# Ten of sixteen tiles transposed by DMA from SyncE, two V weight groups interleaved, and every load of the first stage in one queue

## The reference

```python
def reference(x, w_q, w_k, w_v, w_o, w_gate, w_up, w_down):   # x: 4 x 2048 x 2048, f32
    x = x + _layernorm(attn(_layernorm(x), w_q, w_k, w_v, w_o))
    x = x + _layernorm(ffn(_layernorm(x), w_gate, w_up, w_down))
    return x
# attn: q, k, v = x @ w_q.T, x @ w_k.T, x @ w_v.T; 16 heads of 128;
#       softmax(q k^T / sqrt(128)) v, then @ w_o.T
# ffn:  (silu(x @ w_gate.T) * (x @ w_up.T)) @ w_down.T, 8192 hidden channels
```

## Time and profile before

| | us |
|---|---|
| median of three runs | 2283.08 |
| all three runs | 2280.57, 2641.86, 2283.08 |
| the profiled execution, its own time | 2280.66 |
| its span, slowest core (core 6) | 2278.8 |
| spans of the eight cores | 2276.7 to 2278.8 |
| PE busy in the span | 2240.6 (98%) |

### The profile page before, as it was taken

One profiled execution on the slowest core, in us unless ns is written; L12 is line 12 of the kernel. 1 busy time (PEld: TensorE's weight loads), 2 busy tenths in 40 slices (PEclk: granted clock), 3 DMA queues, 4 the chain that ended last, 5 costly groups with the idle time before them and its releaser, 6 DMA issues.

```text
span 2278.8 us, 26636 instructions; the slowest of 8 cores (2276.7 to 2278.8 us)
## 1 busy us (share of the span) xinstructions
PE 2240.6 (98%) x10528; PEld 1018.2 (45%) x10528; DVE 573.4 (25%) x771; ACT 567.8 (25%) x743; POOL 132.9 (6%) x252
## 2 busy tenths in 40 slices
PE   5999999999999999999999999999999999999998
PEld 3544444444444444444444444444444444444443
DVE  6400045454554557601000001010000000000005
ACT  4411266666666651200000000000000000000003
POOL 0000000000000000000000000000000010000000
PEclk9999999999999999999999999999999999999999
DMA  9720021411414157654444444444444374445447
GB/s 265 162 44 2 10 35 22 75 28 32 71 23 71 28 111 187 164 93 74 75 80 77 74 75 80 78 74 75 79 78 74 65 145 68 83 66 86 72 83 258
DMA packets 61689, 190.49 MB, mean 84 GB/s; under 512 B 21632, under 2 KB 21632, under 8 KB 56448
## 3 DMA queue, kind: packets, MB, share of 16 engines
q0 software_dynamic: 36864, 134.27, 35.8%
q1 hardware_dynamic: 8064, 50.34, 6.3%
q10 hardware_dynamic: 16640, 4.20, 1.0%
HBM read 302.06 MB, written 16.78 MB: 140 GB/s over the span
## 4 chain that ended last, share of the span: by engine, by line
PE 96%; DMA 1%; issue 1%; ACT 1%; DVE 1%; DVEq 0%; SPq 0%; ACTq 0%; POOLq 0%
PE ps L167 96%; DMA wvs<-wv 1%; DMA xs<-xb 1%; ACT kt L173 0%; DVE st L232 0%; ACT pt L170 0%; ACT pvc L173 0%; DVE xn L240 0%; ACT x L170 0%; ACT sdv L170 0%; ACT ln1t L173 0%; SPq L164 0%; DVE x L831 0%; DVE fs L814 0%; DVEq L849 0%
## 5 line engine op out<-in xcount | busy, mean ns | idle before, releaser
L167 PE MATMUL ps<-ln3t,we 128*128 128x512 bf16 x3872 | 835.9, 379 | 0.0
L167 PEld LDWEIGHTS ps<-ln3t,we 128*128 128x128 bf16 x3872 | 378.9, 98 | 456.8
L167 PE MATMUL ps<-ln1t,w 128*128 128x512 bf16 x1536 | 371.7, 379 | 3.3 <-ACT kt L173 3.3
L170 ACT ACTIVATE pt<-ps,kon 128x1024 bf16<-128x1024 f32 x256 | 285.1, 1115 | 190.4 <-PE ps L167 190.4
L170 ACT ACTIVATE sil<-ps 128x512 f32<-128x512 f32 x128 | 76.3, 597 | 780.0 <-PE ps L167 779.6
L167 PEld LDWEIGHTS ps<-ln1t,w 128*128 128x128 bf16 x1536 | 148.1, 98 | 190.1 <-issue 15.5
L167 PE MATMUL ps<-wvs,ln1t 128*128 128x512 bf16 x1024 | 225.3, 381 | 6.3 <-DMA wvs<-wv 6.3
L167 PE MATMUL ps<-ring,ga 128*128 128x512 bf16 x1024 | 222.1, 379 | 0.4
L167 PE MATMUL ps<-ring,gb 128*128 128x512 bf16 x1024 | 221.7, 379 | 0.0
L167 PEld LDWEIGHTS ps<-wvs,ln1t 128*128 128x128 bf16 x1024 | 100.0, 98 | 125.6 <-issue 9.3
L167 PEld LDWEIGHTS ps<-ring,ga 128*128 128x128 bf16 x1024 | 100.0, 98 | 121.9 <-issue 1.8
(11 more groups left out here) (59 smaller groups left out, 895.2 us busy)
## 6 DMA issues: line engine op xcount, KB each, us to landing
ring<-wd POOLq DMA_DIRECT2D x64, 512.0 KB, 6.0
we<-wu POOLq DMA_DIRECT2D x61, 512.0 KB, 5.9
we<-wg POOLq DMA_DIRECT2D x60, 512.0 KB, 6.0
xs<-xb SPq DMA_DIRECT2D x16, 1024.0 KB, 14.8
wvs<-wv POOLq DMA_DIRECT2D x16, 512.0 KB, 11.9
w<-wq POOLq DMA_DIRECT2D x16, 512.0 KB, 6.1
w<-wk POOLq DMA_DIRECT2D x16, 512.0 KB, 6.0
xr<-xb SPq DMA_DIRECT2D x8, 1024.0 KB, 7.1
```

Of the source, the lines that this page charges most:

```text
L167: return op("t", lambda e: e.matmul(dst, lhsT, rhs, start=start, stop=stop), ctr)
L170: return op("s", lambda e: e.activation(dst, src, fn, bias=bias, scale=scale), ctr)
```

## The change

It does the following:

- Tiles 6 to 15 are no longer transposed by PE and ACT. DVE writes them into a ring of four buffers XNB, and SyncE issues a DMA transpose of each (`x_transpose_dma`) from XNB into LN1T. From tile 10 on the norm waits until the transpose four tiles back has landed.
- x is loaded by GpSimd, in one queue with the weights. The weights of groups 0 and 1 no longer wait for a tile of x; their place in the list sets their order. SyncE issues nothing in this stage but the ten transposes.
- PE multiplies tiles 0 to 5 with group 0, then tiles 0 to 3 with group 1 piece by piece, and then in turn tile k of group 0 and tile k-2 of group 1. The first two tiles of group 2 are done piece by piece.
- From tile 6 on DVE does the first block of the next tile's statistics while it waits for the square root. The order before, in which from tile 7 on the whole statistics of a tile stood ahead of the norm of the tile before it (`x_norm_behind`), is gone.

```diff
--- before.py
+++ after.py
@@ -91,6 +91,7 @@
     XS = [at("xs%d" % i, o, 2048, F32) for i, o in enumerate(
         (OT_O, OT_O + 8192, OT_O + 16384, VT_O + 49152, VT_O + 57344))]
     XN = at("xn", OT_O + 24576, 4096, BF16)
+    XNB = at("xnb", VT_O + 32768, 8192, BF16)
     W = at("w", W_O, 6144, BF16)
     WV = at("wvs", R_O, 16384, BF16)
     KT = at("kt", R_O, 4096, BF16)
@@ -181,7 +182,6 @@
 
     dI = C("dI")
     vK = C("vK")
-    k_ident = dma("g", IDENT.r(0, 128), idn[:, :], dI)
     op("v", lambda e: e.memset(ONES.r(0, 128), 1.0))
     op("v", lambda e: e.memset(KON.r(0, 1), EPS))
     k_const = op("v", lambda e: e.memset(KON.r(1, 1), -SH), vK)
@@ -199,6 +199,7 @@
     sSD = C("sSD")
     vRS = C("vRS")
     vXN = C("vXN")
+    dLT = [C("dLT%d" % i) for i in range(4)]
     tT = C("tT")
     sT = C("sT")
     tV = C("tV")
@@ -210,8 +211,8 @@
 
     def x_load(tc):
         if tc >= 5:
-            wt("y", xnorm[tc - 5])
-        x_in[tc] = dma("y", XS[tc % 5].r(0, 2048), xb[tc * 128:(tc + 1) * 128, :], dX[tc % 5])
+            wt("g", xnorm[tc - 5])
+        x_in[tc] = dma("g", XS[tc % 5].r(0, 2048), xb[tc * 128:(tc + 1) * 128, :], dX[tc % 5])
 
     def row_aggr(p):
         wt("v", (vB, vB.n))
@@ -225,21 +226,36 @@
         wt("v", rs)
         return rs
 
-    def x_stats(tc):
+    def x_stats(tc, blocks):
         p, xs = tc % 2, XS[tc % 5]
         wt("v", x_in[tc], aggr.get(tc - 2))
-        for c in range(4):
+        for c in blocks:
             op("v", lambda e, c=c: e.bn_stats(ST.r(p * 24 + c * 6, 6), xs.r(c * 512, 512)), vB)
+
+    def x_norm(tc):
+
+        p, xs = tc % 2, XS[tc % 5]
+        x_stats(tc, range(1 if tc >= 7 else 0, 4))
         aggr[tc] = row_aggr(p)
-
-    def x_norm(tc):
-        p, xs = tc % 2, XS[tc % 5]
+        if 6 <= tc < NTC - 1:
+            x_stats(tc + 1, range(1))
         row_rstd(p, aggr[tc])
-        if tc >= 2:
-            wt("v", xt_pe[tc - 2])
+        if tc >= 6:
+            dst = XNB.r((tc - 6) % 4 * 2048, 2048)
+            wt("v", lnt.get(tc - 4) if tc >= 10 else None)
+        else:
+            dst = XN.r(p * 2048, 2048)
+            wt("v", xt_pe.get(tc - 2))
         xnorm[tc] = op("v", lambda e: e.tensor_scalar(
-            XN.r(p * 2048, 2048), xs.r(0, 2048), MV.r(p * 2, 1), SDV.r(p * 2 + 1, 1),
+            dst, xs.r(0, 2048), MV.r(p * 2, 1), SDV.r(p * 2 + 1, 1),
             ALU.subtract, ALU.mult), vXN)
+
+    def x_transpose_dma(tc):
+
+        wt("y", xnorm[tc])
+        lnt[tc] = op("y", lambda e: e.dma_start(
+            LN1T(tc * 128, (2048, NKC), (1, 128)), XNB.r((tc - 6) % 4 * 2048, 2048), transpose=True),
+            dLT[tc % 4], 16)
 
     def x_transpose(tc):
         if tc == 0:
@@ -259,12 +275,10 @@
 
     wv_in = {}
 
-    def wv_load(g, after=(None, None, None, None)):
-
-        for c in range(4):
+    def wv_load(g, chunks=range(4)):
+        for c in chunks:
             if g >= 2:
                 wt("g", v_pe[(NTC - 1, g - 2)])
-            wt("g", after[c])
             wv_in[(g, c)] = dma("g", WV.r((g % 2) * 8192 + c * 2048, 2048), wv[g, c, :, :], dWV[g % 2][c])
 
     v_pe = {}
@@ -303,55 +317,85 @@
         src = wq if m % 2 == 0 else wk
         w_in[m] = dma("g", W.r((m % 3) * 2048, 2048), src[m // 2, :, :], dW[m % 3])
 
-    def x_norm_behind(tc):
-
+
+    x_load(0)
+    k_ident = dma("g", IDENT.r(0, 128), idn[:, :], dI)
+    for c in range(4):
+        x_load(c + 1)
+        wv_load(0, [c])
+
+    def x_next(tc):
         if tc < NTC:
-            x_stats(tc)
-        x_norm(tc - 1)
-        if tc + 4 < NTC:
-            x_load(tc + 4)
-
-    for tc in range(5):
-        x_load(tc)
-    wv_load(0, [x_in[tc] for tc in range(4)])
-
-    def x_at_once(tc):
-        x_stats(tc)
-        x_norm(tc)
-        x_load(tc + 5)
-
-
-    for tc in range(4):
-        x_at_once(tc)
+            x_norm(tc)
+            if tc + 5 < NTC:
+                x_load(tc + 5)
+
+
+    x_next(0)
+    x_transpose(0)
+    x_next(1)
+    v_part(0, 0, 0)
+    x_transpose(1)
+    x_next(2)
+    v_part(1, 0, 0)
+    for tc in (2, 3):
+        for t in range(tc - 1):
+            v_part(t, 0, tc - 1)
         x_transpose(tc)
-        if tc:
-            for t in range(tc):
-                v_part(t, 0, tc - 1)
-            for c in range(tc):
-                v_part(tc, 0, c)
-    x_at_once(4)
-    x_transpose(4)
-    x_at_once(5)
-    for t in range(4):
+        x_next(tc + 1)
+        v_part(tc - 1, 0, tc - 1)
+        for c in range(tc):
+            v_part(tc, 0, c)
+    for t in range(2):
         v_part(t, 0, 3)
         v_out(t, 0)
-    for k in range(4, NTC):
-        if k == 4:
-            x_at_once(6)
-            x_stats(7)
-        elif k + 3 <= NTC:
-            x_norm_behind(k + 3)
-        if k + 1 < NTC:
-            x_transpose(k + 1)
+    x_transpose(4)
+    x_next(5)
+    for t in range(2, 4):
+        v_part(t, 0, 3)
+        v_out(t, 0)
+    v_part(4, 0, 0)
+    v_part(4, 0, 1)
+    v_part(4, 0, 2)
+    x_transpose(5)
+    wv_load(1, [0])
+    x_next(6)
+    x_transpose_dma(6)
+    v_part(4, 0, 3)
+    v_out(4, 0)
+    wv_load(1, [1, 2, 3])
+    for tc in range(7, 10):
+        x_next(tc)
+        x_transpose_dma(tc)
+        if tc == 7:
+            v_proj(5, 0)
+        else:
+            for t in range(4):
+                v_part(t, 1, tc - 8)
+    for c in (2, 3):
+        for t in range(4):
+            v_part(t, 1, c)
+            if c == 3:
+                v_out(t, 1)
+    for k in range(6, NTC):
+        if k + 4 < NTC:
+            x_next(k + 4)
+            x_transpose_dma(k + 4)
         v_proj(k, 0)
-    wv_load(1, [x_in[tc] for tc in (7, 9, 11, 13)])
-    wt("g", x_in[NTC - 1])
+        v_proj(k - 2, 1)
     for m in range(3):
         w_load(m)
-    for g in (1, 2, 3):
-        if g >= 2:
-            wv_load(g)
-        for tc in range(NTC):
+    for k in (NTC - 2, NTC - 1):
+        v_proj(k, 1)
+    for g in (2, 3):
+        wv_load(g)
+        if g == 2:
+            for c in range(4):
+                for t in range(2):
+                    v_part(t, g, c)
+            v_out(0, g)
+            v_out(1, g)
+        for tc in range(2 if g == 2 else 0, NTC):
             v_proj(tc, g)
```

More of the change, by code:

```diff
@@ L226, in row_rstd @@
         return rs
-    def x_stats(tc):
+    def x_stats(tc, blocks):
         p, xs = tc % 2, XS[tc % 5]
         wt("v", x_in[tc], aggr.get(tc - 2))
-        for c in range(4):
+        for c in blocks:
             op("v", lambda e, c=c: e.bn_stats(ST.r(p * 24 + c * 6, 6), xs.r(c * 512, 512)), vB)
-        aggr[tc] = row_aggr(p)
     def x_norm(tc):
         p, xs = tc % 2, XS[tc % 5]
+        x_stats(tc, range(1 if tc >= 7 else 0, 4))
+        aggr[tc] = row_aggr(p)
+        if 6 <= tc < NTC - 1:
+            x_stats(tc + 1, range(1))
         row_rstd(p, aggr[tc])
-        if tc >= 2:
-            wt("v", xt_pe[tc - 2])
+        if tc >= 6:
[4 more added lines that the diff above has]
+            wt("v", xt_pe.get(tc - 2))
         xnorm[tc] = op("v", lambda e: e.tensor_scalar(
-            XN.r(p * 2048, 2048), xs.r(0, 2048), MV.r(p * 2, 1), SDV.r(p * 2 + 1, 1),
+            dst, xs.r(0, 2048), MV.r(p * 2, 1), SDV.r(p * 2 + 1, 1),
             ALU.subtract, ALU.mult), vXN)
+    def x_transpose_dma(tc):
[3 more added lines that the diff above has]
+            dLT[tc % 4], 16)
     def x_transpose(tc):
```

## The result

The changed kernel takes **2315.43 us**, median of 13 executions (lowest 2288.23), against 2283.08 us before (2280.57 the lowest). The ratio is **1.0109, 95% interval 1.0077 to 1.014**: within 2% as forecast, but the time is 29 us above the predicted 2286.6 us and outside 2274 to 2296.

A forecast was written before the change was run, and what follows sets the result against it. PE (98% busy) bounds the kernel, DMA the first stage to about 55 us. Tile 6 at 79.4 us, 1.7 of clock, 186.6 of sums and 0.8 end the stage at 268.5 against 265.0: +3.5, forecast 2286.6 us, range 2274 to 2296.

The forecast's parts named there:

- Loads and w_v: First stage: 3.1 us per load, group 1's first piece at 54.9 us, PE waiting about 8 us from near 47 us.
- Tile 6's transpose: First stage: starved packet for packet beside loads, landing at 79.4 us when PE needs it at 72.2 us.
- The 0.4 us for the signal in the sum: Added for the signal to the landing time of tile 6's DMA transpose, 79.4 us.
- DVE, tile 15, weights of group 2: After tile 6: DVE idle before tile 10's norm, tile 15 and weights loading from about 83 us, 0.8 us exposed for group 2.
- The stage's end: End of the first stage, where the next one's first matmul starts: 268.5 us against 265.0, +3.5 us.
- Slow clock. I charge 1.7 us once.: PE at 1.2 GHz behind the wait for tile 6: 1.7 us once, between 0 and 3 us possible.
- pacing by the transposes: Rival, first stage: 11.7 us per transpose, one following the other, sets PE's pace; +45 us, 2328 us; chance 0.04.
- another wait: Rival: an unseen wait, such as DVE or SyncE held by a full ring at 80 to 100 us; +8 to +20 us; chance 0.11.
- Transposes in time: Rival: tile 6 landed by 72.2 us without holding up loads, stage ending at 259.6 us; -5.4 us, 2277.7 us; chance 0.28.

The follow-up runs named there:

- after_again: The changed kernel run again unaltered, to trace an execution with a long pair of cores; 2319.74 us, ratio 1.0132.
- hold_loads: Changed kernel with loads of tiles 12 to 15, and q and k weights behind them, held until tile 9's transpose landed; 2284.55 us, 1.0004.
- busy_pe: Changed kernel with 28 and 30 idle matmuls filling PE's waits for group 1's first piece and tile 6's transpose; 2287.91 us, 1.003.
- busy_second: Changed kernel with 30 idle matmuls only where PE waits for tile 6's transpose; 2288.95 us, 1.004.
- pe_all: Changed kernel with all sixteen tiles transposed by PE, none by DMA in the stage; load order and single queue kept; 2285.96 us, 1.0017.
- dma_from_10: Changed kernel with tiles 6 to 9 transposed by PE and only tiles 10 to 15 by DMA; 2286.87 us, 1.0019.
- dma10_late_w: Changed kernel with only tiles 10 to 15 transposed by DMA, q and k weights loaded only behind tile 15's transpose; 2280.56 us, 0.9989.
- dma10_act: As dma10_late_w, but the six DMA transposes issued from ACT's queue in place of SyncE's; 2281.22 us, 0.9986.
- pe_all_gap: pe_all with one added PE wait, for tile 14's load ahead of tile 6's sum with group 0; 2292.42 us, 1.0036.
- busy_first: Changed kernel with 28 idle matmuls only where PE waits for group 1's first piece; 2312.98 us, 1.0116.
- after_mixed: Changed kernel with 16 idle PE transpositions behind each of the first six pairs of sums after the wait for tile 6's transpose; 2317.1 us, 1.0119.
- hold_wait: hold_loads with an added PE wait for tile 9's DMA transpose ahead of tile 6's sum with group 0; 2320.59 us, 1.018.
- pe_all_wait6: pe_all with PE waiting for tile 14's load ahead of the last piece of group 1 of tile 1, earlier than pe_all_gap; 2319.64 us, 1.0164.
- before_gap: Kernel before the change with one added PE wait, for tile 14's load ahead of tile 7's first sum; 2298.01 us, 1.0072.
- before_two_gaps: Kernel before the change with two added PE waits: tile 10's load ahead of tile 5's first sum, tile 14's ahead of tile 7's; 2300.68 us, 1.0083.
- pe_all_wait7: pe_all_gap with PE waiting for tile 15's load in place of tile 14's; 2299.04 us, 1.0073.
- hold_wait_long: hold_wait with PE waiting for tile 12's load in place of tile 9's transpose; 2297.28 us, 1.0087.
- dma10_wait7: dma_from_10 with an added PE wait for tile 15's load ahead of tile 6's sum with group 0; ratio 1.0093.

## Why the prediction was wrong

Step by step, on the profiled execution's slowest core:

- **Loads and w_v.** First piece of group 1 predicted at 54.9 us, PE went on at 56.8; loads took 3.2 us each, the upper bound I had kept. PE's wait was 6.0 us, not 8: it came to it later, held up by ACT's copies between the first tiles (4.9 us in six waits), which I had counted at nothing. Nearly right.
- **Tile 6's transpose.** Predicted: issued at 46.3, landed at 79.4 by one packet for one and a dry queue at the end, PE waiting about 7 us. Measured: issued at 49.0, landed at 80.0, wait 6.7 us, 271 packets against 269. Right, in cause and size. (The 0.4 us for the signal in the sum has no row behind it, and no run measures it alone.) The Trainium skill's page "DMA: Bandwidth & Descriptors", section "SWDGE vs HWDGE vs iDMA", names packets of preferably up to 4096 bytes as the point where an engine changes queue; read as sixteen of the transpose's records per turn, that would have given no wait. The trace disagrees with this reading: a turn was one packet of some 250 bytes (0.25 MB in 1026).
- **DVE, tile 15, weights of group 2.** DVE idle before tile 10's norm 5.4 us, q and k weights issued from 82.6 us, the transposes from tile 8 on landing in 4.6 to 20 us, and 2.8 us of waiting for group 2 where I had 0.8. PE waits for no transpose after tile 6. Right, with the last term 2 us short.
- **The stage's end.** 268.5 us predicted, 267.1 to 274.5 measured: +2 to +10 us, core by core, instead of +3.5. On the profiled slowest core (272.7) the 4.2 us missing are 0.9 at the transpose, 1.2 of clock and 2.0 at group 2, 4.1 in all.
- **"Slow clock. I charge 1.7 us once." This step failed.** I priced what a wait does to the clock from a single wait of 2.50 us, and put between 0 and 3 us around it. The 0.50 that I looked for came, 5.7 us of it behind the second wait on this core (80.3 to 86 us), 2.9 us lost. What came on top was no part of any row before: in six of ten executions the granted clock then fell to 0.81 on a pair of cores for some 161 us (traced in after_again, told from spans and mean clocks in these six), and cost 25 to 30 us. A term that I took for a constant of a wait depends on how long the wait is, and on the execution. The metric is the slowest core, so one pair is enough.

The rivals: pacing by the transposes (2328) did not occur, and "another wait" (2291 to 2303) names no wait that exists; the measured time lies between the two, and neither foresaw anything of the clock. "Transposes in time" was right about the stage's end under its own condition, as hold_loads shows; without the wait the same kernel returns 2284.6 us.

The sum of a median execution: stage +2 to +10 us, the stretch at 0.81 about +27, together some 29 to 37, and 32.4 us measured (2315.43 - 2283.08).

## What to carry to other kernels

A short wait that one adds to a full PE isn't priced by its own length: here one of 5 to 6 us cost 27 us more through the clock in most executions, and one of 10 us did not. So price it by a kernel that has a wait of that length, or fill it with idle matmuls, or make it disappear. A DMA transpose should not be issued beside a full load queue unless its consumer can wait for the whole queue: its small packets pass one for one (269 against 271 in 6 us here, and 31 us to landing in place of 4.3). And look at spans of all cores and of all executions first: the one profiled execution showed nothing of the main cost.

## What the runs showed of the hardware

**A granted clock of 0.81.** Neither 0.50 (1.2 GHz) nor 1.00 (2.4 GHz): steady for 161 to 163 us in each of the 16 traced cores that have it (from 87 to 90 us to 247 to 251 us), with matmuls 0.261 us apart. In the counted executions it comes to both cores of a pair, to one pair up to all four, in some executions and not in others. The second waits on the eight cores of each profiled execution, that is those that end at 74 to 104 us, against its presence:

| second wait on PE | kernels | executions with a long pair |
|---|---|---|
| none, or 1.9 us at most | busy_pe, busy_second, hold_loads, pe_all, dma_from_10 | 0 of 49 |
| none, but 3.2 us on one core | dma10_late_w, dma10_act | 0 of 18 |
| 2.7 to 4.4 us | pe_all_gap | 0 of 9 |
| 3.1 to 6.8 us | the change (two sessions), busy_first, after_mixed, hold_wait, pe_all_wait6 | 23 of 30 |
| 8.2 to 16.0 us (one core of the last kernel a third one of 7.7) | before_gap, before_two_gaps, pe_all_wait7, hold_wait_long | 0 of 21 |
| 18 to 23 us | dma10_wait7 | 0 of 2 |

On the 16 cores at 0.81 the second wait was 4.9 to 6.3 us; the shorter and longer ones of the 23-of-30 row belong to cores that stayed at 1.00. The length is not enough by itself: in the profiled execution of the change all eight cores waited 5.7 to 6.7 us and none has the stretch, and first waits of 6.0 to 6.2 us (ending near 57 us) are followed by some us at 0.50 and then by 1.00 until the second. Nor is the wait wholly needed: in one of 70 counted executions of the kernel before whose cores are on record, a pair ended some 28 us behind at 0.983 (2309.25 us), and in an uncounted one of dma10_late_w a pair some 20 us behind at 0.985; neither was traced.

The Trainium skill's page "TensorE: Matmul & The Clock Gate", "Part 1: The HAM clock gate", says "K is binary" of the clock gate's half and full rate, and names beside it a peak-current limiter that takes a whole die to 13/16 and holds it there while the load lasts. The level here agrees with 13/16 (0.81). The extent does not: in one die of after_again cores 0 and 1 have it and cores 2 and 3, with the same work, do not, and it ends near 250 us while PE stays full. Whether it is that limiter, no run shows. What grants it, why pairs, why not each time, and why first waits don't bring it, stays open. Where the waits end does not tell the kernels apart: those on the cores at 0.81 end at 77.5 to 80.3 us, those of pe_all_gap, too short, at 77.3 to 79.4, those of before_two_gaps, too long, at 75.8 to 80.0. The place of a wait of the critical length was not varied.

**Late cores in the output projection.** Executions with DMA transposes in the first stage have single cores that lose up to 19 us there, where they should lose nothing. Core 1 of the second profile, about 930 us and about 955 us, and ACT's two transposes there (their landing in the last row; the earlier trace rows has 11.7 us at most):

```profile
930.00:940.00 10.00, 10.00 (x48) 4.53 (x47) 8.82 (x15) 2.61 (x5) 0.53 (x1) 1.00 1.55 73
...
950.00:960.00 10.00, 1.72 (x5) 0.63 (x6) 2.14 (x5) 2.93 (x5) 0.00 (x0) 0.54 1.17 158
```

```profile
L687 ACTq DMA_TRANSPOSE ln3t<-xn x2: 4256/10656/17056, 924.1 to 939.2; - x2
...
DMA to landing us min/median/max: 30.6/32.1/33.6
```

The DMA engines are full by share while they move 73 GB/s, the transposes land after 31 to 34 us, ACT is held, and PE waits 11.6 us for it. On the profiled cores of pe_all and pe_all_wait7 the longest such landing is 10.4 us, and no core is late there; in hold_loads and hold_wait one core each has one of 37.2 and 41.2 us. Issuing the first stage's transposes from ACT in place of SyncE left one core of dma10_act at 2282.5 us beside seven at 2273.1 to 2278.5, but that core was late already in the first stage, so the run decides nothing on it. The cause is open.
